# First attention written out in 16 slots, with scores in four row groups and split output projection

## The reference, cut to what matters

```
def body(S, xs):
    qb, kb, vb = xs
    scores = jnp.einsum('bhid,bhjd->bhij', qb, kb) * intra_decay[None]
    o_intra = jnp.einsum('bhij,bhjd->bhid', scores, vb)
    o_inter = jnp.einsum('bhid,bhde->bhie', qb * q_decay[None, :, :, None], S)
    S_new = blk_decay[None, :, None, None] * S + jnp.einsum('bhjd,bhje->bhde', kb * k_decay[None, :, :, None], vb)
    return (S_new, o_intra + o_inter)
...
qkv = (x @ Wqkv + bqkv).reshape(B, N, 3, H, hd)
...
return out @ Wout + bout
```

## Time and profile before

| | us |
|---|---|
| median of 3 runs | 2586.15 |
| the profiled execution's own time | 2579.9 |
| its span, from first to last instruction | 2578.1 |
| first projection of the first attention | 40.45 |
| first DMA of the next stage | 448.25 |

### The profile page before, as it was taken

How to read it: one execution, slowest core, us unless ns; L and a number is a source line. 1 busy time by engine, 2 the same in 40 slices (tenths; PEclk the granted TensorE clock), 3 DMA queues, 4 the chain that set the end, 5 groups by cost and what they waited for, 6 DMA issues and landing times. The chain is left out here.

```text
span 2578.1 us, 52965 instructions
## 1 busy us (share of the span) xinstructions
PE 2266.5 (88%) x21584; PEld 1566.7 (61%) x21584; DVE 1449.1 (56%) x2103; ACT 868.2 (34%) x1804; POOL 425.4 (16%) x374
## 2 busy tenths in 40 slices
PE   4988987899999799968888888888986997999997
PEld 3565654677777578843444444444444886788886
DVE  4433423333322534538888888888885333676665
ACT  4232221322222230015555555555554221211114
POOL 0000000121122115430111111111111000322221
PEclk9999999899999899988999999999999998999999
DMA  4011010700000653332333433343333661211111
GB/s 141 1 65 64 2 49 24 248 23 18 25 8 0 230 183 118 120 117 65 91 99 78 109 93 97 83 116 85 92 87 98 224 229 51 56 31 28 33 37 65
DMA packets 169261, 217.90 MB, mean 85 GB/s; under 512 B 36624, under 2 KB 108368, under 8 KB 165360
## 3 DMA queue, kind: packets, MB, share of 16 engines
q1 hardware_dynamic: 168208, 213.62, 27.3%
q10 hardware_dynamic: 864, 1.57, 0.2%
HBM read 143.76 MB, written 71.37 MB: 83 GB/s over the span
## 5 line engine op out<-in xcount | busy, mean ns | idle before, releaser
L1380 ACT ACTIVATE a_prob<-ps,a_nmax 128x256 f32<-128x256 f32 (+7 forms) x512 | 377.0, 739 | 365.0 <-DVE a_nmax L1408 230.4
L1490 PE MATMUL ps<-a_kt,a_q 64*128 64x512 f32 (+5 forms) x1536 | 381.1, 537 | 104.7 <-ACT a_prob L1380 84.4
L1408 DVE TENSOR_REDUCE a_nmax<-ps 128x1 f32<-128x1024 f32 (+3 forms) x256 | 256.5, 1002 | 103.5 <-PE ps L1490 103.0
L1490 PEld LDWEIGHTS ps<-a_kt,a_q 64*128 64x128 f32 x1536 | 143.7, 194 | 202.2 <-ACT a_prob L1380 124.9
L1422 DVE STREAM_TRANSPOSE a_pt_long<-a_prob 128x1024 f32<-128x1024 f32 (+3 forms) x256 | 257.9, 1022 | 0.0
L1504 PE MATMUL ps<-a_pt_long,a_v 32*64 32x256 f32 (+3 forms) x7808 | 227.1, 342 | 0.4 <-DVE a_pt_long L1422 0.2
L1504 PEld LDWEIGHTS ps<-a_pt_long,a_v 32*64 32x64 f32 x7808 | 153.3, 131 | 100.8 <-issue 75.0
L1457 POOL TENSOR_TENSOR a_o<-a_left 128x256 f32<-128x256 f32 x128 | 90.4, 728 | 610.8 <-ACT a_left L1390 610.8
L50 PE MATMUL ps<-f_w_hi,f_hT_hi 128*128 128x512 f32 x432 | 168.5, 390 | 3.6 <-POOL f_hT_lo L1801 3.6
L51 PE MATMUL ps<-f_w_lo,f_hT_hi 128*128 128x512 f32 x432 | 168.6, 390 | 0.0
L52 PE MATMUL ps<-f_w_hi,f_hT_lo 128*128 128x512 f32 x432 | 168.0, 389 | 0.0
(11 more groups left out here) (212 smaller groups left out, 4353.4 us busy)
## 6 DMA issues: line engine op xcount, KB each, us to landing
a_q<-scratch_QT SPq DMA_DIRECT2D x512, 64.0 KB, 2.1
scratch_QT<-k_qo SPq DMA_DIRECT2D x64, 256.0 KB, 2.3
a_v<-scratch_V SPq DMA_DIRECT2D x64, 256.0 KB, 4.7
scratch_OT<-a_o SPq DMA_DIRECT2D x32, 512.0 KB, 3.2
o_of<-scratch_OT SPq DMA_DIRECT2D x32, 512.0 KB, 4.5
f_packed<-in_packed SPq DMA_DIRECT2D x11, 768.0 KB, 6.0
a_kt<-scratch_KT SPq DMA_DIRECT2D x128, 64.0 KB, 4.0
f_scale<-in_scale SPq DMA_DIRECT2D x11, 384.0 KB, 6.1
```

The costliest lines, as they stand in the source:

```text
L1380: last = nc.scalar.activation(prob[:, n % PRING, s].rearrange("p (a w) -> p a w", w=w), SC[n % 2][:, a, 0:w], ACT.Exp, bias=nmax[:, n % 4, ...
L1408: nc.vector.tensor_reduce(nmax[:, n % 4, 0:1], SC[n % 2][:, :, 0:width(0, t)], AX.XY, ALU.max, negate=True).then_inc(maxed, 1)
L1490: last = pe.matmul(sc[:, a, 0:w], q[r, slot, heads[a * hf], :], kt[r, b, keys], start=not masked, stop=True, skip_group_check=True)
```

## The change

Only `attention0` changes (and its constant tables: two are gone, and the bias of V is added as a row). It is written out without a loop, in 16 slots (chunk c, group g, number i = 4c + g).

- **Scores.** `qe` is gone. Each head's scores are a matmul of its own, with 32 partitions of weights (`kT[r, cols]`) and 32 of moving `qT[r, cols]`, 128 columns. The four heads use four row groups of the array and four PSUM banks `A`. The queries are copied once.
- **Values.** V is projected with tokens on the output partitions, all heads at once (`values`, 48 matmuls for each chunk, in the slot of g = 0). It isn't turned any more.
- **States.** They are kept as 32 columns a head (`state[P, HG, 5, 32]`), without the mask. K by V is 4 matmuls of 32x32 outputs a tile, and the state's part of the output is 4 matmuls, each with 32 partitions of weights and 32 output partitions, all four into bank `O`. A chunk that ends a sequence computes no last state, and the first tile of a sequence has no state's part.
- **Output projection.** `Wout` and the attention's output are split in high and low parts: 12 float32r matmuls a tile (`finish`) in place of 4 of float32. The low part of the output is made by GpSimd. It is done for chunk c - 1 in slot g = 1 of chunk c, and for the last chunk at the end.
- **Order.** Group i - 1 is attended in slot i, behind the projections of K and Q of group i. The next chunk's x is turned one quarter a slot; the router's logits and V come in slot g = 0, the choice in g = 1, the mask's turn at the end of g = 3.
- **Start.** The tables' inputs go on ScalarE's queue and the weights on SyncE's, in thirds: K first, then Q, then V. The tables are made first, then the third of K is split, then x, then the third of Q; V's third is split in slot 0 and `Wout` in slot 1.
- **Banks.** One bank `TR` for everything that is turned (before: three, and one of `A`), so each user of it waits for the reader of the one before.

The diff, cut to its core:

```diff
...
-                            nc.tensor.matmul(A[n % 2].rearrange("p (h i) -> p h i", i=P), kT[:, b, s * P:(s + 1) * P],
-                                             qe[:, b, :, s * P:(s + 1) * P], start=True, stop=True
-                                             ).then_inc(scores.sem, 1)
...
+    G_USES = []
+    for c, g, i in slots():
+        G_USES += [("K", i), ("Q", i)]
+        if g == 0:
+            G_USES += [("V", c * TPC + t) for t in range(TPC)] + [("L", c)]
+        if g == 1 and c:
+            G_USES += [("Y", (c - 1) * TPC + t) for t in range(TPC)]
+    G_USES += [("Y", (NCH - 1) * TPC + t) for t in range(TPC)]
...
+                def outputs(i):
+                    act.wait_ge(o_done, i + 1)
+                    if i:
+                        act.wait_ge(o_lo, i)
+                    nc.scalar.activation(of[:], O, ACT.Copy).then_inc(o_out, 1)
+                    act.wait_ge(o_out, i + 1)
+                    if i >= HG:
+                        act.wait_ge(gemm, projected("Y", (i // HG - 1) * TPC + TPC - 1))
+                    nc.scalar.activation(oT[0][:, i % HG, :], of[:], ACT.Copy).then_inc(o_hi, 1)
...
+                for c, g, i in slots():
+                    keys(i)
+                    if i == 0:
+                        split_third(2)
+                        act.wait_ge(zeroed, 2)
+                        nc.scalar.activation(wr[0][:, :, 0:16], wr_stage[:], ACT.Copy).then_inc(w_hi, 1)
+                    if g == 1:
+                        exponents(c)
+                    if g >= 2 and c + 1 < NCH:
+                        high(c + 1, g)
+                    queries(i)
+                    if i:
+                        outputs(i - 1)
+                    else:
+                        root(1)
+                    if i == 1:
+                        act.wait_ge(wo_in, 16)
+                        for k in range(KC):
+                            nc.scalar.activation(wout[0][:, k, :], xb[:, k, :], ACT.Copy).then_inc(w_hi, 1)
+                    if g == 0:
+                        logits(c)
+                    if g < 2 and c + 1 < NCH:
+                        high(c + 1, g)
+                    if g == HG - 1:
+                        if c + 2 < NCH:
+                            root(c + 2)
+                        masks(c)
...
+                def advance(c, g, i):
+                    dve.wait_ge(kv_prod, i + 1)
+                    if i >= HG:
+                        dve.wait_ge(o_done, i - HG + 1)
+                    before = states_until(c, g) - kept(c)
+                    for s in range(kept(c)):
+                        n = step(c, s)
+                        new, kv = state[:, g, (n + 1) % 5, :], TR[:, s * HD:(s + 1) * HD]
+                        if n == 0:
+                            nc.vector.tensor_copy(new, kv).then_inc(states, 1)
+                        else:
+                            if s:
+                                dve.wait_ge(states, before + s)
+                            else:
+                                dve.wait_ge(states, states_until(c - 1, g))
+                            nc.vector.scalar_tensor_tensor(new, state[:, g, n % 5, :], bdecay[:, g:g + 1], kv,
+                                                           ALU.mult, ALU.add).then_inc(states, 1)
...
+                def decay_scores(i):
+                    g = i % HG
+                    if i:
+                        dve.wait_ge(o_done, i)
+                    dve.wait_ge(scored, i + 1)
+                    for s in range(TPC):
+                        nc.vector.tensor_tensor(am[:, s, :].rearrange("p (h w) -> p h w", h=4),
+                                                A_ALL[:, :, s * P:(s + 1) * P], decay[:, 4 * g:4 * g + 4, :], ALU.mult
+                                                ).then_inc(decayed, 1)
...
+                for c, g, i in slots():
+                    if g == 1:
+                        maxima(c)
+                    if g >= 2 and c + 1 < NCH:
+                        low(c + 1, g)
+                    decay_queries(i)
+                    token_keys(i)
+                    if i == 0:
+                        split_third(2, Q_LO)
+                        dve.wait_ge(zeroed, 2)
+                        dve.wait_ge(w_hi, WR_LO)
+                        nc.vector.tensor_tensor(wr[1][:, :, 0:16], wr_stage[:], wr[0][:, :, 0:16].bitcast(F32),
+                                                ALU.subtract).then_inc(w_lo, 1)
+                        dve.wait_ge(w_lo, V_LO)
+                    if g == 0:
+                        token_values(c)
+                    if g == 1 and c:
+                        add(c - 1)
+                    advance(c, g, i)
+                    decay_scores(i)
+                    if i == 0:
+                        statistics(1)
+                        normalise(1)
+                    if i == 1:
+                        for k in range(KC):
+                            dve.wait_ge(w_hi, WR_LO + k + 1)
+                            nc.vector.tensor_tensor(wout[1][:, k, :], xb[:, k, :], wout[0][:, k, :].bitcast(F32),
+                                                    ALU.subtract).then_inc(w_lo, 1)
+                    if g == 1:
+                        choose(c)
+                    if g < 2 and c + 1 < NCH:
+                        low(c + 1, g)
+                    if g == HG - 1 and c + 2 < NCH:
+                        statistics(c + 2)
+                        normalise(c + 2)
+                add(NCH - 1)
...
+                def multiply(c, g, i):
+                    pe.wait_ge(k_tok, i + 1)
+                    if g == 0:
+                        pe.wait_ge(v_out, TPC * (c + 1))
+                    for s in range(kept(c)):
+                        for h in range(4):
+                            last = pe.matmul(TR[32 * h:32 * h + 32, s * HD:(s + 1) * HD],
+                                             ktok[:, s * P + 32 * h:s * P + 32 * h + 32],
+                                             vtok[:, c % 2, s, g * P + 32 * h:g * P + 32 * h + 32], start=True, stop=True,
+                                             skip_group_check=True)
+                    last.then_inc(kv_prod, 1)
...
+                def score(i):
+                    pe.wait_ge(qT_out, i + 1)
+                    if i:
+                        pe.wait_ge(decayed, TPC * i)
+                    for s in range(TPC):
+                        cols = slice(s * P, (s + 1) * P)
                         for h in range(4):
                             r = slice(32 * h, 32 * h + 32)
+                            last = pe.matmul(A[h][:, cols], kT[r, cols], qT[r, cols], start=True, stop=True,
+                                             skip_group_check=True)
...
+                def attend(i):
+                    c, g = divmod(i, HG)
+                    if i:
+                        pe.wait_ge(o_out, i)
+                    pe.wait_ge(qd_out, i + 1)
+                    pe.wait_ge(states, states_until(c, g))
+                    for s in range(TPC):
+                        cols, n = slice(s * P, (s + 1) * P), step(c, s)
+                        if n:
+                            for h in range(4):
+                                r = slice(32 * h, 32 * h + 32)
+                                pe.matmul(O[r, cols], state[r, g, n % 5, :], qd[r, i % 2, cols], start=True, stop=False,
+                                          skip_group_check=True)
+                        pe.wait_ge(decayed, TPC * i + s + 1)
+                        for h in range(4):
+                            r = slice(32 * h, 32 * h + 32)
+                            last = pe.matmul(O[r, cols], vtok[:, c % 2, s, g * P + 32 * h:g * P + 32 * h + 32],
+                                             am[:, s, h * P:(h + 1) * P], start=n == 0, stop=True, skip_group_check=True)
+                    last.then_inc(o_done, 1)
...
+                pe.wait_ge(first_in, 32)
+                for k in range(KC):
+                    turn_x(0, k)
+                pe.wait_ge(w_lo, K_LO)
+                pe.wait_ge(xt_lo, KC)
+                for c, g, i in slots():
+                    if g == 0 and c:
+                        pe.wait_ge(xt_lo, KC * (c + 1))
+                    project("K", c, g)
+                    if i:
+                        pe.wait_ge(states, states_until(*divmod(i - 1, HG)))
+                    if g == 1:
+                        pe.wait_ge(lg_out, c + 1)
+                        if c + 1 < NCH:
+                            pe.wait_ge(xt_lo, KC * (c + 1) + 1)
                         for t in range(TPC):
+                            last = nc.tensor.transpose(TR[:, t * 16:(t + 1) * 16], lgT[:, t * P:(t + 1) * P],
+                                                       ident[0:16, 0:16])
+                        last.then_inc(lg_turned, 1)
+                    if g >= 2 and c + 1 < NCH:
+                        if g == 2:
+                            pe.wait_ge(xt_lo, KC * (c + 1) + 2)
```

(39 more changed lines are left out.)

775 lines of the change are left out of this document (333 added, 442 removed).

## The result

| us | before | changed |
|---|---|---|
| median | 2585.62 (2583.15 to 2587.84, 4 runs) | 2475.39 (2474.42 to 2479.34, 4 runs) |
| the profiled execution's own time | 2579.9 | 2475.74 |
| its span | 2578.1 | 2473.9 |
| first projection | 40.45 | 27.45 |
| first DMA of the next stage | 448.25 | 341.45 |

The ratio is 0.9581, with a 95% interval of 0.9569 to 0.9593. The forecast was 2494, with a range of 2466 to 2535: right in sign and inside the range. The gain is 110 us by the medians where 92 were forecast. The stage itself became 106.8 us shorter (448.25 - 341.45, forecast 92.3).

What follows compares the result with a forecast made beforehand. TensorE, busy for 88% of the span, was taken as the bound. Hand-over: 62.7 (slot 1 begins) + 255.2 (slots 1 to 15) + 14.8 (waits) + 2.8 (slow matmuls) + 20.5 (end) = 356.0 against 448.25, so 2494 us; range 2466 to 2535.

Steps and rivals of the forecast that it cites:

- The start: Before slot 1: first projection at about 25.7 us, V's third split until 38.2, slot 1 begins at 62.7.
- State's part: In attend, four matmuls of 32 partitions to 32 partitions: 0.35 us a token tile, between bounds of 0.21 and 0.85.
- rival 1: State's part runs one head after the other because of the shared bank: 0.85 us a tile, +28 us, 2522; chance 0.14.
- K by V: In each slot, 28 passes on average of 32 columns: 0.85 us, between bounds of 0.55 and 2.8.
- The allowance of 9 us: Added over slots 1 to 15, 0.6 a slot: four more changes of tile form at 0.1 and one hand-over of 0.2.
- Waits inside: TensorE's stalls after slot 1 begins, mostly through bank TR in slots g = 2, longest in slot 2: 14.8 us together.
- Projections: In slots 1 to 15, matmuls at 0.23 us: K and Q 5.5 a slot, V and logits 41.4, output projection 33.1.
- The end: After the last slot: attend 2.8, copy and splits 3.0, output projection 11.0, last add and store 3.7; 20.5 us.
- rival 2: No row groups overlap: scores stay at 0.85 us a tile too, +34 us on top, 2556; chance 0.04.
- Rival 3: Hand-overs bind the slot: waits for each reader of bank TR lose 1.8 us more a slot, +27, 2521; chance 0.13.
- Rival 4: Waits at the start and inside cost 16 us less, since transfers land earlier: 2478; chance 0.12.
- Rival 5: Slower: all 1408 score, state and K by V passes drain the array before the next, +212 us, 2706; chance 0.03.

Runs made afterwards that it cites:

- e5: The changed kernel with the second chunk's statistics and normalising ahead of slot 0's state steps and decays on VectorE: 2469.61 us, 0.9554 of the kernel before.
- e7: The changed kernel with V's third of the weights split before slot 0's own work: 2473.43 us, 0.9573 of the kernel before.
- e9: The changed kernel with the zero-padded score matmul of before, ScalarE's four padded copies behind the copy of the queries: 2520.04 us, 0.9757 of the kernel before.
- e10: The changed kernel with each group's four state parts ahead of its value parts; output not the whole sum: 2461.56 us, 0.9536 of the kernel before.
- e4: The changed kernel with x's next low part ahead of the choice, and its high part ahead of Wout's split: 2466.10 us, 0.9544 of the kernel before.
- e6: The changed kernel with each group attended at the end of its own slot, not a slot later: 2499.64 us, 0.9673 of the kernel before.
- e1: The kernel before with its chunk loop written out on all engines: 2586.36 us, 1.0011 of the kernel before.
- e12: The changed kernel with e4, e5, e7, e10, the first root ahead of the tables, and one start flag a bank and quadrant: 2437.43 us, 0.9435 of before.

## Why the prediction was right, and where its sizes were off

**The bound.** TensorE sets the stage, and the forecast as a difference of one point held: the part behind it moved by 2.6 of 110 us, with no change of code. The sum was 14.6 us too high at the hand-over (356.0 against 341.45). Part of that nearness is luck: the terms below that were too high make 27.5 us, those that were too low 13.0. By steps:

- **The start: 3.1 us too low.** Forecast were the first projection at 25.7 and slot 1 at 62.7; they came at 27.45 and 65.81. The tables began at 12.49 and not at 10, the root came at 20.05 and not at 18.4, and the normalised x was ready at 22.5 and not at 20.5. Behind that VectorE's queue sets the first projection, and not a bank (chunk 0's x is turned into the four banks `A`): it splits K's third behind the normalising, and not meanwhile as forecast, and then makes the low part of x, without a gap.

```profile
22.42 2.49 DVE L390 TENSOR_TENSOR a_wqkv_lo<-a_vtok,a_wqkv_hi 128x512 fp32r<-128x512 f32 x4
24.83 2.48 DVE L395 TENSOR_TENSOR a_xt_lo<-ps,a_xt_hi 128x512 fp32r<-128x512 f32 x4
```

In slot 0, V began at 39.83 and not at 38.2, behind nine projections of some 0.63 us each, and with twelve of its own matmuls at the lower clock (0.50, 5.26 us for the twelve) V and the logits took 16.5 us and not 13.8. Against that, VectorE's chain to the normalised x took 6.5 us and not 8.5, and a turn of x at the lower clock (0.50) added 1.4. Both waits of slot 0 were named rightly, and e5 and e7 show them.
- **Scores: 1.35 forecast, 1.10 to 1.23 measured**, 3.2 us too high. The row of the second attention that I scaled by two was the right one; e9 shows what they are worth.
- **State's part: 0.35 a tile forecast and measured** (the attends of slots 1 to 15 came to 38.2 us for 39.2). Four row groups that write one bank, each its own partitions, overlap: one after the other was estimated at 0.85 a tile, and L634 takes 0.35 here and 0.25 in e10. That was the open question of the prediction, and rival 1 is out.
- **K by V: 0.85 forecast, 0.41 for 32 passes and 0.30 for 24.** This is 7.5 us over 15 slots, and it is an error of choice: the lower bound of 0.55, from the nearest row, was itself too high, since that row's passes have 128 columns and these have 32.
- **The allowance of 9 us** for changes of form and hand-overs was counted twice, and is the largest error: a change costs some 0.13 (e10), but the measured 0.35 for L566 that I used already held it. The turns of x and the small turns were another 1.7 too high.
- **Waits inside: 14.8 forecast, 9.5 measured.** Named rightly: slot 2 is the longest (5.6 forecast, 4.3 measured), and the other two of g = 2 are 2.1 and 1.9 (2.8 forecast). The choice takes 2.1 us in VectorE's queue (83.01 to 85.13), where I had read 3.0 off the kernel before. e4 removes these waits, as it must by the queue that the prediction names.
- **Projections: 8.4 us too low.** The 684 matmuls of slots 1 to 15 took 168.2 us, where 157.0 and 2.8 for those at the lower clock were put. The pace is 0.2326 and not 0.23 us (1.8), the first of each of 31 blocks takes 0.11 more (3.4), and the longer matmuls cost 5.7 and not 2.8: beside the two priced waits the lower clock (0.65 from 231.80 to 236.70) came behind one of only 1.9 us in slot 10.
- **The end: 1.5 us too low** (21.95 against 20.5, from the last attend at 319.50). The wait for the low part by GpSimd, 2.7 us, was priced; the slower clock behind it (granted 0.91 over the last 19 us, seven matmuls at 0.43) wasn't.

The terms of slots 1 to 15 (19.1 too high, net) outweigh the 3.1 and 1.5 that were too low.

**The rivals.** Rival 1 and rival 2 are out by L634 and L619. Rival 3 (hand-overs in every slot) is out: 9.5 us of waits in 15 slots. Its mechanism is real, though, and e6 is the kernel that has it: 26.4 us of short waits. Rival 4 had the right sign (its 2478 is near the result), but not its reason: the start came later and not sooner, the waits inside were only 5.3 us less, and the rest was work that took less time. Rival 5 is out: 1408 small passes take 49.2 us (18.8 + 23.6 + 6.8), 0.035 each.

**What stays open.** The experiments price the scores (41 us), the delay by a slot (22), the split projection (4 to 6) and, by e1, the loops (0). The rest of 107 (the start's 13, V by tokens, the boundary waits of 14.2, K by V) wasn't undone one by one, and the effects needn't add up.

## What to carry to other kernels

Price a block of small matmuls by their columns and by how many tiles stand side by side, with one change of form for the block (0.13 us in e10); then group the passes of one form, and set the start flag once for a bank and quadrant, as e12 does. Attend (or do whatever needs another engine's answer) one step late, so that TensorE always has a projection between question and answer. When the stage is bound by one engine, list its remaining waits with what stands ahead of the awaited instruction in the other engine's queue: four such reorderings, with not one instruction fewer, gave 27 us in the profiled stage and 22 in the median here, more than their idle time, since the engine also ran slowly behind each long wait (granted clock 0.50 to 0.58). And compare two traces slot by slot: where a slot differs that no edit touches, that part of the difference isn't the edit's.
